# A second attention layer rewritten: separate PSUM banks, division behind the value product, a list of steps per engine

## What is computed

```python
q = hidden_state @ Wq + bq                     # 32 heads of 16
k = encoder_hidden_state @ Wk + bk             # 8 heads of 16
v = encoder_hidden_state @ Wv + bv
scores = jnp.einsum('bkgld,bksd->bkgls', q, k) * scale + mask
attn = jax.nn.softmax(scores, axis=-1)
out = jnp.einsum('bkgls,bksd->bkgld', attn, v) @ Wo + bo
x = out + hidden_state
return (x - mean(x)) * rsqrt(var(x) + EPS) * gamma + beta
```

## Time and profile before

| | us |
|---|---|
| three runs: median (lowest to highest) | 1234.41 (1229.36 to 1235.71) |
| the profiled execution | 1230.13 |
| its span, first to last instruction | 1228.3 |
| second layer within the span | about 856 to 1228 |
| PE, DVE, ACT, POOL busy over the span | 88%, 59%, 53%, 33% |

### The profile page before, as it was taken

The page is one execution under the profiler, slowest core; times in us unless marked ns, Lnnn a source line. Parts: engine busy times, 40 slices in busy tenths (PEclk is TensorE's granted clock), DMA queues, the critical chain, the costliest instruction groups (busy, mean ns, idle before and its releaser), DMA issues.

```text
span 1228.3 us, 27299 instructions
## 1 busy us (share of the span) xinstructions
PE 1082.4 (88%) x8912; PEld 910.8 (74%) x8912; DVE 720.4 (59%) x2795; ACT 655.0 (53%) x2188; POOL 405.3 (33%) x539
## 2 busy tenths in 40 slices
PE   5999999999999983999999999998488888888863
PEld 4788888888888873898998999997366666666642
DVE  4577777677777764721222222222389898888982
ACT  4455555555455543733333333333388787888871
POOL 1233333333333331100000000000047676767674
PEclk9999999999999997999999999999699999999996
DMA  6312211111112102610110110040311212111100
GB/s 252 89 38 74 64 45 45 45 45 45 45 47 72 41 10 61 223 52 1 53 51 4 47 51 24 28 121 30 90 49 47 65 45 64 47 62 54 56 18 18
DMA packets 65348, 71.09 MB, mean 58 GB/s; under 512 B 7056, under 2 KB 41104, under 8 KB 65296
## 3 DMA queue, kind: packets, MB, share of 16 engines
q1 hardware_dynamic: 65296, 70.42, 18.3%
HBM read 49.43 MB, written 20.97 MB: 57 GB/s over the span
## 4 chain that ended last, share of the span: by engine, by line
PE 55%; POOL 14%; DVE 12%; issue 11%; ACT 4%; DMA 2%; SPq 1%; POOLq 1%; DVEq 0%; ACTq 0%
PE J L162 31%; PE S L162 15%; POOL pr L690 9%; POOL stat L710 3%; DVE pr L937 3%; PE S L1146 3%; PE O L1161 2%; ACT pr L792 2%; PE S L1128 2%; DVE stat L991 2%; POOL fin L720 1%; DVE stat L989 1%; DVE res L972 1%; DVE V L895 1%; PE T L1103 1%
## 5 line engine op out<-in xcount | busy, mean ns | idle before, releaser
L690 POOL TENSOR_TENSOR pr<-pr,rec 128x512 f32<-128x512 f32 x256 | 260.9, 1040 | 395.2 <-DVE rec L948 395.2
L792 ACT ACTIVATE pr<-pr,nmax 128x128 f32<-128x128 f32 (+1 forms) x768 | 324.5, 428 | 21.0 <-DVE nmax L937 20.9
L937 DVE CUSTOM_DVE_ANT_0 pr<-S,madd 128x128 f32<-128x128 f32 (+1 forms) x768 | 205.3, 330 | 13.4 <-PE S L1128 9.3
L1322 ACT ACTIVATE g_m<-J,b_part_m 128x256 f32<-128x256 f32 x128 | 60.6, 474 | 217.9 <-PE J L162 217.9
L1146 PE MATMUL S<-ident,pr 128*128 128x128 f32 x1024 | 130.4, 276 | 20.2 <-DVE nmax L937 16.7
L792 ACT ACTIVATION_READ_ACCUMULATOR pr<-pr,nmax 128x1 f32 x768 | 147.0, 191 | 0.0
L1146 PEld LDWEIGHTS S<-ident,pr 128*128 128x128 f32 x1024 | 115.3, 142 | 32.8 <-POOL pr L690 25.7
L1299 POOL TENSOR_TENSOR resid_m<-resid_m,b_all_m 128x512 f32<-128x512 f32 x16 | 23.1, 1464 | 325.3 <-DMA resid_m<-in_x 325.3
L954 DVE COPY pT<-S 128x512 f32<-128x512 f32 x128 | 84.1, 685 | 7.3 <-PE S L1146 5.9
L800 ACT ACTIVATE pT<-S 128x512 f32<-128x512 f32 x128 | 71.9, 587 | 24.8 <-PE S L1146 24.8
L162 PE MATMUL J<-nT0hi_m,uphi_m 128*128 128x256 f32 x256 | 73.1, 286 | 9.7 <-DVE uplo_m L150 8.9
(11 more groups left out here) (189 smaller groups left out, 2831.1 us busy)
## 6 DMA issues: line engine op xcount, KB each, us to landing
staged<-in_L_xattn_mlp_w SPq DMA_DIRECT2D x16, 512.0 KB, 4.7
rows<-in_ctx SPq DMA_DIRECT2D x16, 256.0 KB, 2.8
rows<-in_x SPq DMA_DIRECT2D x16, 256.0 KB, 3.0
kept_c<-hThi SPq DMA_DIRECT2D x16, 256.0 KB, 2.6
kept_c<-hTlo SPq DMA_DIRECT2D x16, 256.0 KB, 2.8
kept_n<-n_out SPq DMA_DIRECT2D x16, 256.0 KB, 2.4
n_in<-kept_n SPq DMA_DIRECT2D x16, 256.0 KB, 3.7
resid_m<-in_x SPq DMA_DIRECT2D x16, 256.0 KB, 2.8
```

The source lines that it names most:

```text
L690: pool.tensor_tensor(part, part, by.unsqueeze(2).broadcast_to([P, per_bank, keys]), ALU.mult).then_inc(normed, 1)
L792: last = nc.scalar.activation(part, part, ACT.Exp, bias=nmax[slot][:, at], scale=-1.0, accum_out=den[slot][:, at])
L937: last = nc.vector.tensor_tensor_reduce(pr[slot][:, j, cols], S[j][:, cols], madd[s][:, :], -1.0, FAR, ALU.add, ALU.min, nmax[slot][:, j * ...
L1322: nc.scalar.activation(g[slot][:, :], J[j][:, 0:PR], ACT.Gelu_apprx_tanh, bias=b1_part[:, f, :]).then_inc(J_taken[j], 1)
```

## The change

Only the second layer is replaced: `second_attention` stands in place of `attention` with L = 1. The arithmetic of the projections, scores, softmax and norm is the same, apart from these points.

- Banks: S0 to S3 hold only scores. The turned probabilities go to O and T, alternating by group k = 0 to 7 (a group is one bank of scores, four heads). J0 and J1, now G0 and G1, hold projections, spread reciprocals and value products.
- The exponentials are transposed undivided. DVE inverts the 16 sums of a round spread over 16 columns each (256 columns), PE transposes that (`inverse`), ACT copies it to SBUF (`spread`), and DVE multiplies the value product by it (`attended`). POOL then makes the high and low halves.
- Moments use bn_stats and bn_aggr.
- `pr` has eight buffers, one per group, and `pT` two.
- Each engine has its own written list of steps per period; waits are counted from the entry's number. Scores, probs, exp and maximum are steps per group, no longer per pair of banks.

The lists, which are what sets the order (b is the period's entry, `before` b-1, `after` b+1; guards for missing entries left out):

```diff
-        attention(nc, top, staging, 1, ident, handed, banks, x, ctx_rows, add_mask, bq,
-                  (bk, bv), bo, gamma, beta, out)
+        second_attention(nc, top, staging, ident, handed, banks, add_mask, bq, bk, bv, bo, gamma, beta, out)
...
+                def scores(e, r):
+                    if r == 0:
+                        pe.wait_ge(k_ready, e.count(1, 1))
+                    wait(pe, masked, e.count(STEPS, SB * r))
...
+                def probs(e, k):
+                    t = k % 2
+                    pe.wait_ge(exped, e.count(STEPS, k + 1))
+                    wait(pe, copied[t], e.count(SB, k // 2))
...
+                def inverse(e, r):
...
+                    pe.wait_ge(rec_ready, e.count(ROUNDS, r + 1))
+                    for c in range(RC):
+                        mm = nc.tensor.transpose(G[r][:, c * R:(c + 1) * R], rec[r][:, c * EIGHT:(c + 1) * EIGHT, :],
+                                                 ident[:, :])
+                    mm.then_inc(r_full, 1)
...
+                def invert(e, r):
+                    dve.wait_ge(exped, e.count(STEPS, SB * r + SB))
+                    nc.vector.reciprocal(rec[r][:, :, :], den[r][:, :].unsqueeze(2).broadcast_to([P, RC * EIGHT, DH1]))\
+                        .then_inc(rec_ready, 1)
...
+                def attended(e, r):
+                    dve.wait_ge(o_full, e.count(ROUNDS, r + 1))
+                    wait(dve, a_ready, e.count(ROUNDS, r - 1))
+                    dve.wait_ge(r_spread, e.count(ROUNDS, r + 1))
+                    nc.vector.tensor_tensor(an[r][:, :], G[r][:, 0:RC * R], inv[r][:, :], ALU.mult)\
+                        .then_inc(a_scaled, 1)
...
+                    if half == 0:
+                        pe.wait_ge(a_scaled, e.count(ROUNDS, 2))
+                        wait(pe, c_ready, min(e.n + 3, B) if e.it is None else e.count(1, 3))
```

More of the change, by code:

```diff
@@ L1191, in _, with __init__, plus, exists @@
                                               finish=finish, projected=projected))
+class Entry:
+    def __init__(self, n, it=None):
+        self.n, self.it, self.s = n, it, n % 2
+    def plus(self, d):
+        return Entry(self.n + d, self.it)
+    def exists(self):
+        return self.it is not None or 0 <= self.n < B
+    def count(self, per, more=0):
+        fixed = self.n * per + more
+        return fixed if self.it is None else self.it * (2 * per) + fixed
+    def uses(self, per):
+        fixed = (self.n // 2 + 1) * per
+        return fixed if self.it is None else self.it * per + fixed
+    def index(self):
+        return self.n if self.it is None else self.it * 2 + self.n
```

485 lines of the change are left out of this document (added).

## The result

The changed kernel takes 1281.0 us (median of four runs, 1279.8 to 1282.75), the kernel before 1235.06 in the same session (1229.36 to 1235.78): the ratio is 1.0387, with a 95% interval of 1.0357 to 1.0417. It is slower by 46 us. The profiled execution took 1279.8, its span is 1278.0. One number further down needs a note: of nine executions of the run narrow_fill, one was a slow one of 1529.75 us at a mean granted clock of 0.69, and its ratio leaves it out.

A forecast was written before the change was run, and what follows sets the result against it. DVE bound the old kernel at 20.1 us per entry; afterwards a cycle of waits, 23.1 us, would. Entry 2's keys at 914.6 plus 13 x 23.1, then 31, 11.2 and 1.8, gave 1258.9, stated as 1260; range 1228 to 1288.

The forecast's parts named there:

- Rival 3: DVE's reciprocal takes eight passes a column, 2.4 us for 256 columns; period 24.6, time 1280 us; chance 0.12.
- Rival 4: PE's clock falls each period after a 2.2 us gap, lengthening query by up to 2.8; period 25.1, 1285 us; chance 0.10.
- the ring: Seven steps of waits across PE, ACT and DVE, from one entry's keys to the next's: 23.1 us per entry.
- The disputed term: DVE's reciprocal over 256 columns, twice per entry: 1.66 us each, a column costing about six times a copied one.
- The wait of the earlier trace: PE held by the probabilities that POOL divides: 1.4 us per entry, forecast to go.
- steps 1, 3, 5 and 6: Keys to scores 1.57; exponentials 6 1.68; high half to third maximum 8.07; scores of round 1 to context 4.99 us.
- step 7: DVE from context through norm, maxima, reciprocal of the next round 0 and copy 4 to the next keys: 4.90 us.
- the tail: From the last entry's keys to the last residual sum: 31 us against 42.9 before.
- the first keys: Low halves of the turned keys of the second layer's first entry on DVE: staying at 871 us.
- Rival 1: The reciprocal costs as other operations, 0.33 us; period 21.2, time 1231 us; chance 0.15.
- step 5: ACT's high half, then DVE's low half, moments, attended, maxima, copy and reciprocal of round 1: 8.07 us.
- rival 2: Faster: the order works and the period falls to about DVE's own sum, 19.0 us; time 1203 us; chance 0.13.

The follow-up runs named there:

- narrow_fill: Changed kernel with the reciprocal taken of the 16 sums alone, then copied wide, plus eight unused matmuls where PE waited: 1242.84 us, ratio 1.0070.
- narrow_second: Changed kernel with the reciprocal of round 1 alone taken of the 16 sums and then spread, round 0 left 256 wide: 1276.48 us, ratio 1.0369.
- early_turn: Changed kernel, order only: turn of entry b+2 ahead of probabilities 5 on PE and of exponentials 6 on ACT: 1238.02 us, ratio 1.0044.
- narrow: Changed kernel with the reciprocal taken of the 16 sums alone in both rounds and a copy to spread it: 1265.27 us, ratio 1.0255.
- best: Changed kernel with all engines' lists rewritten along the cycle of waits, and the reciprocal taken of 16 sums and copied wide: 1208.98 us, ratio 0.9805.

## Why the prediction was right, and where it was off

The forecast was 1260, slower; the measurement is 1281.0, slower, inside the range of 1228 to 1288. It is outside the forecast's own range of 1245 to 1272, though, and next to the prices of rivals 3 (1280) and 4 (1285). The direction and the ring were right by the mechanism. That 1281 still lies in the wide range is owed to the room that was left for these rivals.

**Right: the reciprocal.** The disputed term was 1.66 us, by a line through 4 and 8 columns. Two groups of DVE's in the kernel after, behind the first bar stand the busy time in us and the mean of one in ns:

```profile
L1555 DVE RECIPROCAL rec<-den 128x256 f32<-128x256 f32 x32 | 55.9, 1746 | 0.0
...
L1583 DVE BATCH_NORM_AGGREGATE stat<-stat 128x2 f32<-128x6 f32 x16 | 2.9, 182 | 2.8 <-DVE stat L1580 2.7
```

It lasts 1.746, and the next instruction starts 1.67 behind it (1062.28 to 1063.95). The slope from 8 columns on is (1746 - 193) / 248 = 6.3 ns a column; that is five times a copied column's 1.2, where the prediction said six. bn_aggr, taken at 0.2, is 0.18. The Trainium skill, "VectorE: DVE Perf Modes", section "First, the fixed hardware budget", gives the divide a repeat count of 8; growth with the columns agrees, but the factor in time is five and not eight, and the measurement decides. Rival 3, built on that count, names 1280, the time that came out. It would have been the right number for a wrong reason: its 2.4 us stand nowhere.

**Right: the ring.** Six steps are within 0.2 us, and with the clock held the ring is 23.36 against 23.1. narrow_fill, narrow_second and early_turn show its two ways and its order. The waits stand where they were forecast, in the kernel after between 950 and 1150 us:

```profile
ACT inv L1455 <- PE J L1720: 50.9, 16, 3.5
...
DVE hTlo L1505 <- ACT hThi L1419: 27.4, 9, 3.0
...
PE T L1710 <- ACT pr L1441: 20.3, 9, 2.3
```

The wait of the earlier trace rows is gone, as forecast. ACT's wait before the spread of round 0 is 3.5 and not 2.3: ACT is done with its list sooner than I had summed up. That costs nothing, since what ends the wait is the same.

**Wrong: the clock.** The prediction wanted 1.00 from 900 to 1200 and it was 0.92 in the mean, as it fell once in each period, over the query. Rival 4 is what happened, with the gap of 2.2 us that it had named. Its argument against, that a gap of 2.4 us at 1.00 stood in the earlier trace rows, compared two gaps without what ran around them; the periods of early_turn, alike in their gap and not in their clock, show that a gap's length alone doesn't decide it. But of the 2 us that rival 4 put on the ring only 0.52 came: the query was lengthened by 1.5 us (4.43 for 2.9) instead of 2.8, and of these DVE's own way, with the reciprocal in it, covers one. Over thirteen periods that is 6.8 us.

**Mis-sized.** Each against the forecast: the ring with the clock held +0.26 per period, 3.3 in all, spread over steps 1, 3, 5 and 6, with 0.1 less in step 7; keys of entry 2 behind those of entry 1, 24.6 for 21.6, in a stretch where the clock is low (0.76 from 856 to 914 us); the tail 34.05 for 31; the first keys at 878.4 for 871, of which 5.6 lie before the edit, and 1.9 come from the context, which stands behind turn_query in PE's new list. The keys of entry 1 came 19.2 behind the first, for 22. From the start on the differences are 7.4 - 2.8 + 3.0 + 10.1 (the periods, 6.8 and 3.3) + 3.05 + 0.2 = 20.9, and the span was forecast at 1257.1 and came out at 1278.0.

**What fell with it.** The worth of a cheap reciprocal. Rival 1 had it at 1.9 us per period, at 0.33 a piece. The pair of narrow costs 0.54, and with the clock held it takes 1.54 off (23.36 to 21.82), about what the prediction's ring gives for 0.54: 1.1 in step 5 and 0.5 in step 7. Without that it takes 0.5. In time it is worth 16 us where it stands and 38 less 16, 22, once the clock is held. What the prediction didn't see is how near a better order lay. It gave the faster outcome its price (period 19.0), and best reached 19.25, with the inverse of round 0 in bank T and the narrow reciprocal besides the new order; rival 2's condition, a ring 4 us shorter, was met by another order of the lists and not by cheap handovers.

## What to carry to other kernels

In a kernel whose engines each follow a written list, add up the waits once around from a step of one entry to the same step of the next, over all engines. If that ring is longer than the fullest engine's work, less work on an engine changes little, and an exchange of two steps can change much. Look for the second-longest way beside each part of the ring before pricing an edit: two things side by side pay only together. Here the same separate banks took 1281 us with one order and 1238 with another: what new buffers allow has to be written into the lists. And when an engine's clock falls in a stretch, look at the single periods and not at the mean.

## What the runs showed of the hardware

- A reciprocal of float32 costs by its columns: 168 ns at 4, 193 at 8, 248 at 16, 1746 at 256. Spreading the result with a copy (295 ns for 256 columns) is cheaper than spreading the operand.
- PE's clock fell in each period with a gap of 2.2 us between the turn and the probabilities 7, to a mean of 0.92, and eight unused matmuls in that gap held it at 1.00. In early_turn, with gaps of 1.3 to 1.4 us ahead of probabilities 7 in all periods, it fell in two of thirteen, and in narrow it stayed up in two of thirteen.
- In best the copy of the narrow reciprocal took 0.29 us sixteen times, where POOL ran nothing, and 0.94 or 0.95 thirteen times, each time from 0.48 us after the start of the same product of POOL. That is 0.65 us per period that narrow should have given; whether the ring loses them isn't shown. Timelines of DVE and POOL in best:

```profile
1048.43 0.95 DVE L1563 COPY rec<-few 128x256 f32<-128x256 f32 x1
```

```profile
1047.95 1.28 POOL L1396 TENSOR_TENSOR fin<-nrm,nw_all 128x512 f32<-128x512 f32 x1
1049.31 1.28 POOL L1398 TENSOR_TENSOR fin<-fin,nb_all 128x512 f32<-128x512 f32 x1
```

DVE's copy ends (1049.38) shortly after POOL's first instruction has ended (1049.23). It is the same picture as the 0.94 us for one column in the earlier trace rows, which ends at 978.97; there POOL's two products run from 976.92 to 978.96. The Trainium skill, "SBUF — State Buffer", section "Who interferes with whom", describes a port pair that DVE and POOL share, and that the one which starts first holds for its whole instruction while the other is blocked. The rows agree with this, and no run here tried it by itself.
